# Eight gather passes of a graph network: the short clearing between the list copy and the third gather is left out

## What is computed

```python
# network 1 (twice), network 2 (once)
agg = segment_sum(h[src], dst, num_segments=n)
# network 3 (five layers)
m = relu(h[src] + edge_attr)
agg = segment_sum(m, dst, num_segments=n)
# network 4 (two layers of attention): k[src], v[src], a softmax over the edges of a node, a segment_sum
```

## Time and profile before

| | us |
|---|---|
| median of three runs | 10663.33 |
| lowest and highest | 10651.45, 10667.28 |
| the profiled execution | 10624.18 |
| its span | 10622.3 |
| GpSimd busy in the span | 8301.2 (78%) |
| TensorE busy in the span | 7249.7 (68%) |
| VectorE busy in the span | 5689.4 (54%) |

### The profile page before, as it was taken

The page is one execution under the profiler, slowest core; times in us unless marked ns, Lnnn a source line. Parts: engine busy times, 40 slices in busy tenths (PEclk is TensorE's granted clock), DMA queues, the critical chain, the costliest instruction groups (busy, mean ns, idle before and its releaser), DMA issues. The chain is left out here.

```text
span 10622.3 us, 262820 instructions
## 1 busy us (share of the span) xinstructions
PE 7249.7 (68%) x61807; PEld 6065.5 (57%) x61808; DVE 5689.4 (54%) x14938; ACT 4605.2 (43%) x11428; POOL 8301.2 (78%) x12298
## 2 busy tenths in 40 slices
PE   5536657758866886886886887888555565556565
PEld 3525545537755775775775775776345554455554
DVE  6735544434444555555555555556345557355557
ACT  0023323333324445445445445444455554455564
POOL 2678878878878886885885885885688884788884
PEclk6568878869988998998998998999667777667777
DMA  1245543333325654664664664663455553455553
GB/s 46 76 122 154 154 109 93 92 110 113 112 86 175 188 177 131 193 181 131 187 189 128 186 190 129 183 187 114 140 152 160 159 166 101 132 156 160 158 167 103
DMA packets 1224482, 1511.26 MB, mean 142 GB/s; under 512 B 206845, under 2 KB 806433, under 8 KB 1207894
## 3 DMA queue, kind: packets, MB, share of 16 engines
q1 hardware_dynamic: 1016374, 1055.75, 32.2%
q0 software_dynamic: 207712, 450.99, 16.1%
HBM read 1276.37 MB, written 229.67 MB: 142 GB/s over the span
## 5 line engine op out<-in xcount | busy, mean ns | idle before, releaser
L1987 POOL DMA_INDIRECT rings<-rows_key,pick x2682 | 2689.1, 1003 | 445.7 <-issue 443.0
L2114 PE MATMUL wide<-bigDEF,bigC 128*128 128x128 bf16 (+2 forms) x32256 | 1981.9, 220 | 485.8 <-issue 188.8
L2009 ACT ACTIVATE rings<-iota,pairs 128x128 f32<-128x128 f32 x3576 | 1172.0, 390 | 2593.4 <-PE part L2079 1629.9
L2114 PEld LDWEIGHTS wide<-bigDEF,bigC 128*128 128x128 bf16 x32256 | 1779.7, 103 | 715.7 <-issue 679.8
L1241 POOL DMA_INDIRECT bigDEF<-rows_key_value,idx x1664 | 1654.6, 994 | 286.5 <-issue 231.6
L2079 PE MATMUL part<-rings 128*128 128x128 f32 (+1 forms) x7152 | 1175.4, 305 | 902.4 <-DMA rings<-rows_hidden,pick 257.1
L2225 DVE TENSOR_TENSOR bigDEF<-bigDEF,part 128x128 f32 (+1 forms) x3576 | 1014.5, 284 | 1355.3 <-PE part L2079 518.8
L2079 PEld LDWEIGHTS part<-rings 128*128 128x128 f32 (+1 forms) x7152 | 962.7, 195 | 1078.2 <-issue 1011.3
L1992 POOL MEMSET idle<- 32x448 bf16 (+1 forms) x2392 | 1052.7, 440 | 1.3
L1987 POOL DMA_INDIRECT rings<-rows_hidden,pick x894 | 893.5, 999 | 153.9 <-issue 150.1
L1352 PE MATMUL part<-bigB,rings 128*128 x3328 | 758.6, 399 | 363.5 <-DVE bigDEF L1439 246.5
(11 more groups left out here) (428 smaller groups left out, 12034.4 us busy)
## 6 DMA issues: line engine op xcount, KB each, us to landing
bigC<-sheaf_hots SPq DMA_DIRECT2D x1152, 256.0 KB
rings<-in_attr SPq DMA_DIRECT2D x2235, 64.0 KB
bigC<-sheaf_attr SPq DMA_DIRECT2D x120, 1024.0 KB
walk_value<-bigDEF SPq DMA_DIRECT2D x416, 256.0 KB
rings<-walk_value SPq DMA_DIRECT2D x416, 256.0 KB
rings<-sheaf_steps SPq DMA_DIRECT2D x192, 256.0 KB
sheaf_hots<-bigC SPq DMA_DIRECT2D x192, 256.0 KB
bigB<-sheaf_hots SPq DMA_DIRECT2D x192, 256.0 KB
```

Source lines behind the costliest of these rows:

```text
L1987: e.indirect_dma_start(gbuf[:, draw(n), r, 0:width], None, table, bass.IndirectOffsetOnAxis(ap=c.pick[:, draw(n), r:r + 1], axis=0)).then_ ...
L2009: e.activation(to[:, r, :], c.iota[:, :], ACT.Abs, bias=c.relL[:, bass.ds(q * BUNCH + r, 1)], scale=-1.0).then_inc(c.near.sem, 1)
L2114: last = e.matmul(to, hot, terms, start=x < LOT and x % batch == 0 and j == 2, stop=x >= MARCH - LOT, skip_group_check=True)
```

## The change

`fetch` no longer clears a tile when r is 1, that is after the second gather, where the list copy stands. The copy and the two clearings of 448 stay. One instruction in each bunch goes, on GpSimd alone.

```diff
                     if r == 1:
                         index(i, n + 1)
-                    e.memset(c.rests[r][(LEAD + n) % 2], 0.0)
+                    else:
+                        e.memset(c.rests[r][(LEAD + n) % 2], 0.0)
```

## The result

The kernel got slower, not faster: 10779.17 us (10776.56 to 10781.49, 4 runs) against 10662.19 us before, ratio 1.0117 with a 95% interval of 1.0105 to 1.013. That is 117 us more, where 189 us less were predicted; the time lies above the range. The profiled execution has a span of 10779.6 us.

The account below looks back on a forecast made before the run. GpSimd's program was taken to set the pace in passes 2 to 8. Savings of 65.6 us (passes 2 and 3), 0 (first pass) and 123 us (edge passes), together 189, took 10663 to 10474 us; range 10400 to 10665.

Parts of the forecast that it names:

- What bounds the kernel: In passes 2 to 8 GpSimd runs its program without being stopped and sets the gathers' pace, 4.91 us a bunch.
- Saving of 0.22 us a bunch: On GpSimd, the step from second to third gather falls from 1.53 to 1.31 us, 32.8 us a pass.
- It adds nothing and moves nothing on another engine ... What they hid is only time: Removing the clearings takes away no wait, semaphore or DMA elsewhere; nobody reads the cleared tiles, and GpSimd can do closer gathers.
- Passes 2 and 3, 65.6 us: TensorE waits there for the gathers themselves, so the whole saving arrives: 2 x 32.8 us.
- Passes 2 and 3 at 730 us would overturn the argument as a whole: Test set beforehand: these passes should take 695 to 700 us each for their 447 gathers.
- Edge passes, 123 us less: Passes 4 to 8 gain three quarters of the full saving, 24.6 us each.
- second limit nearby: In edge passes, TensorE's 3.1 us a half before L2114 are not the gathers' and show another limit near.
- Pass 1, nothing: First pass gains 0 (bounds 0 and 32.8 us), its end being set by VectorE and sheaf_steps from HBM.
- Slower: Rival, chance 0.15: closer gathers delay one-hot loads on shared DMA engines; edge passes lose 17 us each or more.
- The third gather did not get longer: Rival, chance 0.06: the third gather, starting earlier, meets other VectorE instructions and lengthens; 73 us saved, 10590 us.
- the pause did not come back: Rival, chance 0.10: the third gather or what follows lasts longer by the clearing's time; nothing changes, 10663 us.
- The range: 10400 us (all of the saving arrives) to 10665 us (no change), leaving out the slower case.

## Why the prediction was wrong

- **What bounds the kernel: right as far as it went.** GpSimd's program did set the pace in passes 2 to 8: with more pause, passes 2 and 3 followed it exactly. What the views could not say is why its program was so long: TensorE without gathers needs 20.0 to 23.1 us a half, so at a pace of 29.2 it had 6 us to spare, and the pauses used them to keep its legs whole.
- **Saving of 0.22 us a bunch: right on GpSimd.** The step from copy to gather came as the earlier trace rows had it, 1.32 us in pass 3 against 1.55:

```profile
2502.98 0.96 POOL L1987 DMA_INDIRECT rings<-rows_key,pick  x1 [0.17 <-issue]
2503.95 0.19 POOL L1981 COPY pick<-pairs 128x3 int32 x1
2504.30 0.98 POOL L1987 DMA_INDIRECT rings<-rows_key,pick  x1 [0.15 <-issue]
```

- **"It adds nothing and moves nothing on another engine ... What they hid is only time": this step failed.** I asked whether something *in a gather* needs the pause and looked at GpSimd alone, in the earlier trace rows, where nothing else ran. The pause served TensorE. In place of the 7.1 and 4.1 us a half that TensorE waited for rows in passes 2 and 3, and that were to shrink by 1.3, it waits 0.4 and 0.2 us for them (8.2 and 3.9 us in 22 halves) and has 4.1 and 2.7 us of gaps in its legs.
- **Passes 2 and 3, 65.6 us: measured 6.** Their full share had been the surest term. "Passes 2 and 3 at 730 us would overturn the argument as a whole" was the right test, and it came out that way (732 and 722 us).
- **Edge passes, 123 us less: measured 87 us more.** VectorE's wait for rows went (87.3 us in the middle of pass 5 to 7.5), as the sum had it, and the 3.1 us a half before L2114, taken for a second limit nearby, were in part this very effect already: in the edge passes the gaps in legs were 1.1 to 1.5 us a half before and fall to 0.15 without gathers. It was a symptom, and I read it as a limit of TensorE's own.
- **Pass 1, nothing: measured 9 us more**, with the same gaps (0.6 to 3.0 us a half).
- **The rivals.** "Slower" had the sign, the 17 us an edge pass, and L2114 as the place, but for another reason. It counted on the DMA engines, and those are cleared: the traffic is the same at 23 us a half, and plain DMAs do no harm. It also let passes 2 and 3 win 66 us. The third gather did not get longer, and the pause did not come back on GpSimd as a whole; but GpSimd's copy began to wait for TensorE (23.1 us in the middle of pass 5, none of note before), the sign that the pace there had passed to TensorE, at a worse value than before (30.8 us a half against 29.7).

```profile
POOL pick L1981 <- PE part L2080: 23.1, 21, 3.0
```

- **The range** took its upper end from "no change" and left out all that was slower; the chance of 0.15 for it was too small for a change that takes away something that does no work of its own.

## What to carry to other kernels

An instruction that computes nothing, on the engine that sets the pace, is a spacing: before taking it away, ask which other engine runs undisturbed because of it, and look there for waits of "issue" inside rows of instructions that have nothing between them. The cheapest test is to leave the suspected work out altogether: TensorE's half fell from 29.2 to 22.8 us without gathers, which no view of waits had shown. When a saving is taken from the engine that sets the pace, the next limit should be priced with that engine running faster, not as it stands.

## What the runs showed of the hardware that I had not expected

- Gathers issued by GpSimd 1.25 to 1.31 us apart, in rows of three and more, stall TensorE's issue elsewhere in the core: 7.1 us of gaps a half in legs that take 12 us. At a mean step of 1.60 us (shortest 1.55) passes 2 and 3 show none of it (0.15 us), at 1.59 us (shortest 1.31) 3.8 and 1.9. The edge passes have 0.9 to 1.4 us even at 1.62. Two gathers 1.28 us apart with a longer step behind them do nothing in pass 3 (0.15 us).
- The price does not go by size: 128 rows of 512 bytes, 128 rows of 64 bytes and 64 rows of 512 bytes give 7.1, 6.8 and 7.2 us of gaps a half in pass 3, and GpSimd itself needs 968, 970 and 930 ns for them.
- A plain DMA of the same size, started by GpSimd, takes it 545 ns and leaves the legs whole (0.13 us of gaps in pass 3; 0.876 of the time of before, against 1.064 with gathers).
- While gathers are this close, GpSimd itself has rare waits of up to 2.9 us before a gather where the profile names nobody; before, in passes 2 to 8, none was over 0.2 us. From the middle of pass 5 of the changed kernel:

```profile
POOL rings L1987 <- issue: 60.1, 315, 2.9
```
